# Self-attention on one core: row sums in fewer, longer blocks, and the negated maxima split between VectorE and GpSimd

## What is computed

```python
scores = jnp.einsum('bqhd,bkhd->bhqk', qh, kh) / jnp.sqrt(jnp.asarray(d, q.dtype))
attn = jax.nn.softmax(scores, axis=-1)
out = jnp.einsum('bhqk,bkhd->bqhd', attn, vh)
```

## Time and profile before

| | us |
|---|---|
| median of three runs | 4140.98 (4130.14 to 4141.34) |
| the profiled execution | 4145.81 |
| its span, first to last instruction | 4144.0 |
| TensorE busy | 3766.3 |
| VectorE busy | 2335.7 |
| GpSimd busy | 2080.8 |
| ScalarE busy | 1877.2 |

### The profile page before, as it was taken

The page is one execution under the profiler, slowest core; times in us unless marked ns, Lnnn a source line. Parts: engine busy times, 40 slices in busy tenths (PEclk is TensorE's granted clock), DMA queues, the critical chain, the costliest instruction groups (busy, mean ns, idle before and its releaser), DMA issues. The chain is left out here.

```text
span 4144.0 us, 51860 instructions
## 1 busy us (share of the span) xinstructions
PE 3766.3 (91%) x19596; PEld 2441.2 (59%) x19596; DVE 2335.7 (56%) x4020; ACT 1877.2 (45%) x3431; POOL 2080.8 (50%) x923
## 2 busy tenths in 40 slices
PE   4699969979999999999999999976999949999998
PEld 2577748844444444444444444425777737888887
DVE  1466642247777777777777777714666525222222
ACT  1465631115666666666666666653555521111111
POOL 0366630005778777787777777765576634000000
PEclk8798879978999999999999999997999869999999
DMA  7566657752130212102131201114666651211110
GB/s 224 139 160 173 169 159 221 226 135 62 26 67 16 64 26 56 37 16 64 26 67 26 59 22 26 31 47 111 145 177 156 163 168 54 73 40 40 40 40 30
DMA packets 213512, 371.45 MB, mean 90 GB/s; under 512 B 36104, under 2 KB 53000, under 8 KB 209704
## 3 DMA queue, kind: packets, MB, share of 16 engines
q1 hardware_dynamic: 213287, 368.49, 33.1%
HBM read 215.54 MB, written 144.51 MB: 87 GB/s over the span
## 5 line engine op out<-in xcount | busy, mean ns | idle before, releaser
L1952 DVE TENSOR_REDUCE a_peak<-a_sm 128x1 f32<-128x512 f32 x2048 | 1276.0, 683 | 448.9 <-PE a_sm L1792 445.4
L1906 ACT ACTIVATE a_e<-a_st 128x512 f32<-128x512 f32 x2048 | 1084.6, 597 | 686.3 <-PE a_st L1814 684.8
L2024 POOL TENSOR_TENSOR a_esum<-a_esum,a_e 128x2048 f32<-128x2048 f32 x256 | 1172.9, 4582 | 127.8 <-ACT a_e L1906 109.2
L1814 PE MATMUL a_st<-a_q,a_k 128*128 128x512 f32 x2048 | 868.3, 427 | 6.7 <-ACT a_e L1906 4.5
L1792 PE MATMUL a_sm<-a_k,a_q 96*128 96x512 f32 x2048 | 831.0, 413 | 47.5 <-DMA a_k<-s_k 28.0
L1814 PEld LDWEIGHTS a_st<-a_q,a_k 128*128 128x128 f32 x2048 | 386.0, 189 | 523.8 <-ACT a_e L1906 256.6
L1827 PE MATMUL a_acc<-a_e,a_v 128*32 128x512 f32 x4096 | 545.5, 605 | 15.1 <-ACT a_sums L1920 14.2
L1792 PEld LDWEIGHTS a_sm<-a_k,a_q 96*128 96x128 f32 x2048 | 396.9, 194 | 145.9 <-DVE a_peak L1952 55.5
L2147 PE MATMUL mlp_ph<-mlp_us,mlp_w_hi 128*128 128x512 f32 x1024 | 336.0, 390 | 32.6 <-DVE mlp_raw_lo L2196 32.6
L2189 ACT ACTIVATE mlp_gelu<-mlp_ph,mlp_b 128x512 f32<-128x512 f32 x128 | 88.3, 690 | 595.7 <-PE mlp_ph L2147 595.6
L2024 POOL TENSOR_TENSOR a_esum<-a_e 128x2048 f32<-128x2048 f32 x32 | 146.8, 4587 | 404.9 <-ACT a_e L1906 404.9
(11 more groups left out here) (151 smaller groups left out, 5171.7 us busy)
## 6 DMA issues: line engine op xcount, KB each, us to landing
p_qs<-s_q SPq DMA_DIRECT2D x192, 256.0 KB, 5.8
s_q<-p_qo SPq DMA_DIRECT2D x64, 512.0 KB, 7.6
a_q<-s_q SPq DMA_DIRECT2D x96, 256.0 KB, 5.0
a_k<-s_k SPq DMA_DIRECT2D x24, 1024.0 KB, 15.5
s_x<-p_x SPq DMA_DIRECT2D x16, 1024.0 KB, 4.3
s_u<-p_ut_hi SPq DMA_DIRECT2D x64, 256.0 KB, 6.0
s_u<-p_ut_lo SPq DMA_DIRECT2D x64, 256.0 KB, 6.5
p_us<-s_u SPq DMA_DIRECT2D x16, 1024.0 KB, 7.8
```

The source lines that it names most:

```text
L1814: pe.matmul(st[0:KR, place(kt, h) % RING], k[:, g % 2, h, kt * P:kt * P + KR], q[:, j % QR, h], start=True, stop=True).then_inc(score_done, 1)
L1906: act.activation(e[0:KR, (j * NKT + kt) % ER, h], st[0:KR, place(kt, h) % RING], ACT.Exp, scale=SCALE).then_inc(score_read, 1)
L1952: dve.tensor_reduce(dst, src, AX.X, ALU.max).then_inc(unit_read, 1)
L2024: pool.tensor_tensor(esum[:], e[:, slot(0)] if x == 1 else esum[:], e[:, slot(x)], ALU.add).then_inc(e_added, 1)
```

## The change

- `POOLED` becomes tiles 0 to 3, 5 to 8 and 10 to 13: GpSimd makes eleven additions, seven ahead of the scaling and four behind it. TensorE adds tiles 4, 9, 14 and 15.
- The narrow products stand in 11 blocks per step instead of 16 (`products`): mostly two units each, at tiles 0, 1, 2, 4, 5, 6, 8, 10, 11, 13 and 15. The partial sum `esum` has a unit of its own (`add_partial`) in the block of tile 1, and only it waits for the additions. `fetch_sums` moves behind the exponentials of tile 1.
- `divide` moves from units 6, 8, 32 to 10, 12, 36.
- `minus_peaks` becomes two reductions with `negate=True` from the same maxima: one rounded to fp32r straight into `neg`, one in full into `minus`. The product with -1, the copy and the subtraction leave VectorE. GpSimd computes `minus` less the rounded part (`lower_parts`), in its queue between the scaling and the last four additions.
- VectorE's next unit 0 waits for the second reduction; `turn_peaks` waits for GpSimd's subtraction.

```diff
-    POOLED = [t for t in range(NKT - 2) if t % 3 != 2] if NKT > 2 else []
+    POOLED = [0, 1, 2, 3, 5, 6, 7, 8, 10, 11, 12, 13]
-    DIVIDE_AT = (6, 8, 32) if NKT > 1 else range(4)
+    DIVIDE_AT = (10, 12, 36)
...
+        def neg_part(x):
+
+            return neg[:, :, 3 * DH:3 * DH + 2 * GH].rearrange("p t (h s) -> p h t s", s=2)[:, :, :, x]
...
-                pe.wait_ge(neg_ready, 2 * (BODY * i + j + 1))
+                pe.wait_ge(neg_lo_ready, BODY * i + j + 1)
...
+            def add_partial(i, j):
+
+                pe.wait_ge(e_added, (BODY * i + j + 1) * ADDS)
+                for h in range(GH):
+                    mm = pe.matmul(acc[h * DH:(h + 1) * DH, 1], ones[0:KR], esum[:, h], start=False, stop=True, tile_position=(0, h * DH))
                 mm.then_inc(tile_used, 1)
+
+            def products(i, j, kt):
+
+                if kt == 0 and exists(i, j - 1):
+                    add_up(i, j - 1, 14)
+                    weigh(i, j - 1, 15)
+                elif kt == 1 and exists(i, j - 1):
+                    add_up(i, j - 1, 15)
+                    add_partial(i, j - 1)
+                elif kt == 2 and exists(i, j):
+                    weigh(i, j, 0)
+                    weigh(i, j, 1)
+                elif kt == 4 and exists(i, j):
+                    weigh(i, j, 2)
+                    weigh(i, j, 3)
+                elif kt == 5 and exists(i, j):
+                    weigh(i, j, 4)
+                elif kt == 6 and exists(i, j):
+                    add_up(i, j, 4)
+                    weigh(i, j, 5)
+                elif kt == 8 and exists(i, j):
+                    weigh(i, j, 6)
+                    weigh(i, j, 7)
+                elif kt == 10 and exists(i, j):
+                    weigh(i, j, 8)
+                    weigh(i, j, 9)
+                elif kt == 11 and exists(i, j):
+                    add_up(i, j, 9)
+                    weigh(i, j, 10)
+                elif kt == 13 and exists(i, j):
+                    weigh(i, j, 11)
+                    weigh(i, j, 12)
+                elif kt == 15 and exists(i, j):
+                    weigh(i, j, 13)
+                    weigh(i, j, 14)
...
-                    if NKT > 1 and kt == 0 and exists(i, j - 1):
+                    if kt == 1 and exists(i, j - 1):
                         fetch_sums(i, j - 1)
...
-                    dve.wait_ge(neg_ready, 2 * (BODY * i + j))
+                    dve.wait_ge(minus_ready, BODY * i + j)
...
-                dve.tensor_scalar(neg_hi[:], top[:], -1.0, None, ALU.mult).then_inc(neg_done, 1)
-                dve.wait_ge(neg_done, n + 1)
...
+                dve.tensor_reduce(neg_part(0), peaks, AX.X, ALU.max, negate=True).then_inc(neg_hi_ready, 1)
+                dve.tensor_reduce(minus[:], peaks, AX.X, ALU.max, negate=True).then_inc(minus_ready, 1)
...
+            def lower_parts(i, j):
+
+                n = BODY * i + j
+                pool.wait_ge(neg_hi_ready, n + 1)
+                pool.wait_ge(minus_ready, n + 1)
+                pool.tensor_tensor(neg_part(1).bitcast(F32), minus[:], neg_part(0).bitcast(F32), ALU.subtract).then_inc(neg_lo_ready, 1)
...
-                    for x in range(1, 6):
+                    for x in range(1, 8):
                         add(i, j, x)
                 if exists(i, j - LATE):
                     scale(i, j - LATE)
+                if exists(i, j + 1):
+                    lower_parts(i, j + 1)
                 if POOLED and exists(i, j):
-                    for x in range(6, len(POOLED)):
+                    for x in range(8, len(POOLED)):
                         add(i, j, x)
```

## The result

The changed kernel takes 4194.57 us (median of four runs, 4190.89 to 4201.37) against 4140.73 for the kernel before: ratio 1.0143, 95% interval 1.013 to 1.0155. It is 54 us slower. I had forecast 4201, 60 more than the median of before.

A forecast was written before the change was run, and what follows sets the result against it. A closed loop through TensorE, VectorE and GpSimd was taken to set the step: 0.07 + 38.2 + 2.2 + 18.64 = 59.1 us against 57.3. Over 31 periods plus end effects, +60 us: 4201 forecast, range 4122 to 4245.

The forecast's parts named there:

- T: The end of a step's last addition on GpSimd, from which the legs of the loop are counted.
- (a): From the step's last GpSimd addition to TensorE's partial sum: 0.07 us.
- (b): TensorE from the partial sum to unit 63 of the next step: 35.6 us, against 39.57 before, without new waits.
- (c): New TensorE waits for VectorE in runs of eight pairs, two with division transposes: 1.09, 0.30, 0.93, together 2.6 us.
- (d): From unit 63 through VectorE's negated maxima, waking GpSimd and its subtraction: 2.2 us.
- (e): GpSimd's four additions queued behind the subtraction: 18.64 us.
- GpSimd alone: Rival: maxima come early enough and GpSimd's own loop of 55.6 us sets the step; about 4095 us, 4%.
- TensorE alone: Rival: TensorE's own pace of 54.0 us sets the step; about 4045 us, 1%.
- The clause on the ring of four slots: Exponentials of tiles 14, 15, 0 and 1 each wait for one of the last four additions to free a slot.
- (1): Rival: the new waits for VectorE do not arise or are absorbed; step 56.5 us, about 4122 us, 15%.
- (3): Rival: half of the waits for VectorE; 4150 to 4180 us, 13%.
- (4): Rival: slower by a clock drop from TensorE standing still (4254 us) or a 1.29 us subtraction (4236 us); together 9%.

The follow-up runs named there:

- experiment 1: Changed kernel with the division's steps after peak units 18, 20 and 42 and the inverse spread after key tile 5: 4154.75 us, ratio 1.0045.
- experiment 2: Changed kernel with GpSimd's subtraction one addition later, behind the eighth instead of the seventh: 4124.02 us, ratio 0.9967.
- experiment 6: Changed kernel with division at 18, 20 and 42, subtraction one addition later, and tile 13 back from GpSimd to TensorE: 4106.70 us, ratio 0.9913.
- experiment 9: Changed kernel with division at 18, 20 and 42, subtraction one addition later, and five exponential slots instead of four, scaling in place: 4095.25 us, ratio 0.9901.
- experiment 10: Changed kernel with five exponential slots instead of four and the scaling in place that makes room: 4218.04 us, ratio 1.0196.
- experiment 3: Changed kernel with division at units 18, 20 and 42 and the subtraction behind the eighth addition: 4094.62 us, ratio 0.9896.
- experiment 4: Changed kernel with the maxima as before: product with -1, copy and subtraction on VectorE, no subtraction on GpSimd: 4260.85 us, ratio 1.0292.
- experiment 8: Changed kernel with the subtraction on VectorE right behind the two negated reductions, and division at 18, 20 and 42: 4217.73 us, ratio 1.0199.
- experiment 7: Changed kernel with GpSimd's subtraction two additions later, behind the ninth: 4227.86 us, ratio 1.0208.

## Why the prediction was right

**The loop (the heart of it).** From T = 1463.76 + 18.71 = 1482.47 the legs are:

| leg | forecast | measured |
|---|---|---|
| (a) T to the partial sum | 0.07 | 0.05 (1482.52) |
| (b) + (c) partial sum to unit 63 | 38.2 | 38.00 (1520.52) |
| (d) unit 63 to the first addition behind the subtraction | 2.2 | 2.22 (1522.74) |
| (e) four additions | 18.64 | 18.68 |
| step | 59.1 | 58.95 |

Experiments 1 and 2 show that it is a loop and not a coincidence: shortening (c) shortens the step by the same amount, and moving the subtraction to a place where it does not wait opens it.

**(c), the waits for VectorE.** Forecast 1.09, 0.30 and 0.93 us. A block of two units and four pairs take 3.93, four more pairs 4 x 0.47: 5.81 without a wait; the three runs took 6.90, 6.19 and 6.79, so 1.09, 0.38 and 0.98. Confirmed, and by experiment 1 also their cause: two of them are for the most part the division's, (1.09 - 0.38) + (0.98 - 0.38) = 1.31 against the 1.33 that the step lost.

**GpSimd.** First addition forecast at T + 2.75, measured 1485.22 = T + 2.75. Idle time ahead of the subtraction forecast as some 3, measured 2.9. The subtraction forecast at 0.2, measured 0.23; its lower bound of 0.17 stands in no row shown. Seven additions with the scaling took longer by 0.38, in which the fourth waits for exponentials of tile 5; that I had not seen, and it lay in the idle time.

**The longest loop, and where I was wrong.** TensorE's own pace was not 54.0 but 56.6, since the waits of (c) belong to it too (experiments 2 and 6). It was still below 59.1, so the forecast stood; my prices for the rivals "GpSimd alone" (4095) and "TensorE alone" (4045) were too low by that: with the maxima off the path the kernel took 4124 (experiment 2). The clause on the ring of four slots named a wait that does not set the step (experiment 9); it holds TensorE back, as forecast, and without it the wait at the partial sum is 2.12 (experiment 10). That TensorE comes to the partial sum 1.5 us early: measured 1.32.

**The sum.** 31 periods gave 52.4 more (forecast 57.1: 0.15 too much in each, and the 3 us that I took off as overlap in the end), the first addition came 1.5 earlier (1.0; 0.4 of it lies ahead of the attention), the last step took 52.55 us (52.6) and so 7.8 more (7.8), and from its last addition to the last scaling it was 0.7 less (0.9). So the last scaling comes 57.9 us later. The median moved by 53.8, the spans of the two profiled executions by only 45.1: from the last scaling to the end of the program it was 1349.5 us instead of 1362.3, in passes that no edit touched. In the profiled executions of all twelve kernels here this stretch lies between 1348.1 and 1362.3, so some ten us in a single pair of executions are not the change's. The 3 us that I took off as overlap stand against the 4.7 (31 x 0.15) too much in the periods, so for the attention the forecast of 60 was 2 us too high; the other 4 by which the median lies under 4201 are of the size of this spread.

**Rivals.** (1) and (3), no or half the waits for VectorE: refuted by the table. (4), the clock: it stayed at 1.00 in the change up to 2760 us, which was the reading of the nearer row, but the danger was close: four of the ten edits brought it about. The standstill that (4) and the reading of the kernel before counted was too large: by the profile TensorE idles 1.2 us per step before (I wrote some 2) and 3.4 in the change, 2.2 more where I wrote 5. The prices of the first rivals are two or three us too high by their own sums (31 x 2.6 off 4201 is 4120, not 4122); nothing hangs on that.

**What held and what did not in the change.** The saving of 3.3 us per step on TensorE came to nothing: above all because of one place in a queue, and in part because the waits for VectorE took 2.6 of it back (TensorE's own pace went from 57.3 to 56.6, not to 54.0). With the subtraction one addition later and the division moved, the same change is 1.0% faster than the kernel before (experiment 3).

## What to carry to other kernels

When an engine with slack gets a new wait in the middle of its queue, follow what is queued behind it back to the wait itself: if it closes a loop, the step is the sum of the loop's legs, whatever each engine's busy share says. A pace for an engine must contain the waits that the edit itself brings, and it must be worked out for every loop, since the second longest is what remains when the first is cut. Work removed between two phases of an engine can be what covered another engine's backlog.

## What the runs showed of the hardware that I had not expected

- A VectorE operation with two SBUF inputs (128x16) that began inside a GpSimd addition took 2.76 us and ended with it; a product with a scalar took 1.88 and ended with it too. Reductions to the same size inside such an addition took 0.21 and 0.22 and were not held (experiments 4 and 8). Why the product, with one tensor as its input, is held where the reductions are not, no run here shows. Negating in the reduction, with output rounded to fp32r, cost nothing: 0.22, as the plain one in the earlier trace rows.
- TensorE's granted clock fell to the lower level, 1.2 GHz, in steps in which it stood still for 2.1 to 3.3 us in one piece: in 30 of 30 in experiment 8, 29 in 4, 18 in 7, 15 in 10. In the change it idles almost as much (94.3% busy between 960 and 2780 us, 94.0% in experiment 10's stretch) but in smaller pieces, 1.32 us in each step at the partial sum, and no fall followed these. The one fall in its attention ahead of the last step came near 2767 us, where the peak units have run out and the largest wait was 1.00, so the length of a single wait is not all of it:

```profile
1540.00:1550.00 10.00, 7.89 (x47) 3.94 (x43) 4.91 (x9) 6.62 (x12) 7.11 (x3) 1.00 0.00 0
...
2760.00:2770.00 10.00, 8.86 (x41) 3.01 (x45) 0.34 (x2) 5.06 (x10) 9.29 (x3) 0.86 0.42 107
```

- Relieving a wait (experiment 10) gained nothing, and the kernel took 23 us more; that TensorE's longer single wait did it, through the clock, is inferred and not shown.
